# Expert weights asked for in another order, a residual written from ScalarE, and two steps of VectorE exchanged

## The reference

```python
scores = softmax(xf @ gate_w.T)                  # 32 experts
top_w, top_i = lax.top_k(scores, 6)              # 6 experts for each token
h  = silu(xb @ w1[e]) * (xb @ w3[e])             # up: 512 -> 352, twice
ob = h @ w2[e]                                   # down: 352 -> 512
y  = zeros.at[token].add(ob * weight)            # back to the tokens
out = x + y + (silu(xf @ sw1) * (xf @ sw3)) @ sw2   # and a shared expert
```

## Time and profile before

| | us |
|---|---|
| median of 3 runs | 1013.27 |
| lowest and highest | 1009.97, 1017.4 |
| the profiled execution's own time | 1011.21 |
| its span, first to last instruction | 1009.2 |

### The profile page before, as it was taken

How to read it: one execution, slowest core, us unless ns; L and a number is a source line. 1 busy time by engine, 2 the same in 40 slices (tenths; PEclk the granted TensorE clock), 3 DMA queues, 4 the chain that set the end, 5 groups by cost and what they waited for, 6 DMA issues and landing times.

```text
span 1009.2 us, 18358 instructions
## 1 busy us (share of the span) xinstructions
PE 977.7 (97%) x5540; PEld 843.5 (84%) x5541; DVE 694.6 (69%) x1053; ACT 592.6 (59%) x966; POOL 270.8 (27%) x170
## 2 busy tenths in 40 slices
PE   8899899999999999999999999989998999999997
PEld 7788698899888987888888888777877898888885
DVE  5655555675567575778766676656667888778876
ACT  6444576666665665455555552542267788778873
POOL 2200221322132141333333220010015455444441
PEclk9899999999999999899999999999999999999999
DMA  9100263312331413222121103510558999998995
GB/s 317 48 0 1 68 219 106 89 52 67 104 95 59 88 43 115 84 84 83 62 83 62 63 21 134 164 43 1 214 198 261 280 307 331 357 345 283 302 346 173
DMA packets 76143, 145.07 MB, mean 144 GB/s; under 512 B 13540, under 2 KB 41060, under 8 KB 75856
## 3 DMA queue, kind: packets, MB, share of 16 engines
q1 hardware_dynamic: 68256, 132.53, 39.2%
q0 software_dynamic: 7856, 12.16, 5.4%
HBM read 146.86 MB, written 15.07 MB: 160 GB/s over the span
## 4 chain that ended last, share of the span: by engine, by line
PE 75%; DMA 8%; SPq 6%; issue 4%; DVE 4%; ACT 3%; DVEq 0%; ACTq 0%; POOLq 0%
PE ps L327 19%; PE ps L328 19%; PE ps L329 19%; PE ps L719 6%; DMA w_raw<-in_w 3%; SPq L954 2%; PE ps L987 2%; PE ps L786 1%; PE ps L796 1%; DMA w_and_lists<-in_w 1%; PE ps L776 1%; PE ps L999 1%; SPq L1193 1%; DMA y_scratch<-x 1%; DMA wo_raw<-in_owT 1%
## 5 line engine op out<-in xcount | busy, mean ns | idle before, releaser
L1012 DVE TENSOR_TENSOR w_l<-w_raw,w_h 128x1408 fp32r<-128x1408 f32 x76 | 121.7, 1624 | 30.0 <-ACT w_h L1008 21.4
L1008 ACT ACTIVATE w_h<-w_raw 128x1408 fp32r (+1 forms) x76 | 102.7, 1377 | 33.1 <-DMA w_raw<-in_w 30.7
L748 POOL TENSOR_TENSOR lw_l<-lw_raw,lw_h 128x1024 fp32r<-128x1024 f32 x32 | 77.0, 2411 | 145.8 <-ACT lw_h L744 140.6
L327 PE MATMUL ps<-w_h,xeT_h 128*128 128x352 f32 x288 | 97.3, 338 | 3.6 <-DVE w_l L1012 3.1
L328 PE MATMUL ps<-w_l,xeT_h 128*128 128x352 f32 x288 | 93.0, 323 | 0.0
L329 PE MATMUL ps<-w_h,xeT_l 128*128 128x352 f32 x288 | 92.9, 323 | 0.0
L1168 POOL DMA_INDIRECT xe<-xn_scratch,take x37 | 40.7, 1100 | 188.4 <-DVE give L1116 100.9
L1172 POOL DMA_INDIRECT y_scratch<-ob,give x34 | 78.6, 2311 | 18.2 <-issue 9.4
L327 PE MATMUL ps<-xT_hi,lw_h 128*128 128x512 f32 x192 | 78.4, 409 | 0.0
L328 PE MATMUL ps<-xT_lo,lw_h 128*128 128x512 f32 x192 | 77.3, 403 | 0.0
L329 PE MATMUL ps<-xT_hi,lw_l 128*128 128x512 f32 x192 | 76.4, 398 | 0.0
(11 more groups left out here) (328 smaller groups left out, 2739.9 us busy)
## 6 DMA issues: line engine op xcount, KB each, us to landing
w_raw<-in_w SPq DMA_DIRECT2D x78, 704.0 KB
w_and_lists<-in_w SPq DMA_DIRECT2D x39, 512.0 KB
w_and_lists<-in_w SPq DMA_DIRECT2D x39, 192.0 KB
rkB<-rk_scratch SPq DMA_DIRECT2D x56, 128.0 KB, 3.2
wq_raw<-in_Wq SPq DMA_DIRECT2D x8, 512.0 KB, 4.9
wo_raw<-in_Wo SPq DMA_DIRECT2D x16, 256.0 KB, 2.9
lw_raw<-in_kwT SPq DMA_DIRECT2D x8, 512.0 KB, 3.4
lw_raw<-in_qwT SPq DMA_DIRECT2D x8, 512.0 KB, 3.4
```

The costliest lines, as they stand in the source:

```text
L327: nc.tensor.matmul(out_ap, lh, rh, start=first, stop=False)
L748: e.tensor_tensor(lw_l[n][:, :, :], lw_raw[n][:, :, :], lw_h[n][:, :, :], ALU.subtract).then_inc(lw_ready[n], 1)
L1008: e.activation(w13_h[:, k, n, :, :], w13_raw[:, slot(raw), n, :, :], ACT.Copy).then_inc(w13_hi_s, 1)
L1012: e.tensor_tensor(w13_l[:, k, n, :, :], w13_raw[:, slot(raw), n, :, :], w13_h[:, k, n, :, :], ALU.subtract).then_inc(w13_ready, 1)
```

## The change

Three edits, all in the routed stage.

1. **Weights.** SyncE asks for the down weights one item later in its list: up weights of item m+5, then down weights of item m+4. In the loop the four values of the item whose down weights come first in a turn (`kept`) are read again from the table, since they can't be carried over from the turn before.
2. **Residual.** The write of `x` is issued by ScalarE, in its pass 2, behind the same wait for `d_read`.
3. **End.** VectorE makes the low half of the last item's result (`ex_dve_ob_low(e, last_i, 1)`) ahead of all four additions of what was read back, not between the second and the third.

```diff
@@ ex_act
             if isinstance(m, int) and m == 2:
                 e.wait_ge(d_read, NSH)
+                e.dma_start(y_dram[0].ap()[0:T, :].rearrange("(t p) d -> p t d", p=P), x[:, :, :]).then_inc(scratch_io, 16)
@@ block.sync
             ex_load_w13(e, 4, 0, 3, values[4])
-            e.wait_ge(d_read, NSH)
-            e.dma_start(y_dram[0].ap()[0:T, :].rearrange("(t p) d -> p t d", p=P), x[:, :, :]).then_inc(scratch_io, 16)
             values += [ex_values(e, m) for m in range(5, 7)]
             for m in (5, 6):
                 ex_load_w13(e, m, m % 2, m // 2 + 1, values[m])
                 ex_load_w2(e, m - 1, (m - 1) % 2, (m - 1) // 2 + 1, values[m - 1])
-            ex_load_w2(e, 6, 0, 4, values[6])
             with e.Fori(1, last_i - 1) as i:
+                kept = ex_values(e, i * 2 + 4)
                 for k in range(2):
                     values = ex_values(e, i * 2 + (k + 5))
                     ex_load_w13(e, i * 2 + (k + 5), 1 - k, i + (k + 3), values)
-                    ex_load_w2(e, i * 2 + (k + 5), 1 - k, i + (k + 3), values)
+                    ex_load_w2(e, i * 2 + (k + 4), k, i + 3, kept)
+                    kept = values
@@ block.vector
-            for t in range(TT):
-                if t == 2:
-                    ex_dve_ob_low(e, last_i, 1)
+            ex_dve_ob_low(e, last_i, 1)
+            for t in range(TT):
                 e.wait_ge(part_arrived[t], 32)
                 e.tensor_tensor(x[:, t, :], y_back[0][:, t, :], y_back[1][:, t, :], ALU.add).then_inc(y_sum, 1)
```

More of the change, by code:

```diff
@@ L1386, in _ @@
                     ex_load_w13(e, i * 2 + (k + 5), 1 - k, i + (k + 3), values)
-                    ex_load_w2(e, i * 2 + (k + 5), 1 - k, i + (k + 3), values)
+                    ex_load_w2(e, i * 2 + (k + 4), k, i + 3, kept)
+                    kept = values
             for k in range(2):
-                for s, n, uses in ((w13_in[k][0], 16, 3 - k), (w13_in[k][1], 16, 3 - k), (w2_in[k], 32, 3 - k)):
+                for s, n, uses in ((w13_in[k][0], 16, 3 - k), (w13_in[k][1], 16, 3 - k), (w2_in[k], 32, 2)):
                     e.wait_ge(s, last_i * n + uses * n)
```

## The result

| | before | after |
|---|---|---|
| median | 1012.79 us (6 runs) | 1027.69 us (6 runs) |
| lowest and highest | 1009.97, 1017.4 | 1024.78, 1029.85 |
| ratio, 95% interval | | 1.0152 (1.0125 to 1.0179) |
| the profiled execution, its span | 1011.21, 1009.2 | 1028.52, 1026.8 |

The change makes the kernel 1.5% slower, some 15 us; 1015 was forecast, with 1022 as the upper end. Lines behind the first edit have moved by one (954 stays, 1193 is now 1194, 1168 is 1169).

A forecast was written before the change was run, and what follows sets the result against it. TensorE's work was taken to bound the first half, with 6.7 us lost to late up weights in the second. Terms 0 + 2.5 - 0.5 = +2.0 us took the profiled execution from 1011.21 to 1013.2; median forecast 1015, range 1007 to 1022.

The forecast's parts named there:

- a turn of its loop that waits for nothing takes 12.42 us: SyncE's loop: two items take 12.42 us; four added reads, 2.62 us, make it 15.04.
- SyncE becomes the bound: Rival, SyncE's loop: turns of 15.5 us, slower than the DMA, give 1021, with the write's worst case 1024; chance 0.20.
- Term 0 for the weights: Weights edit: one item of lead is given and the added reads eat it, net 0 us.
- bounds of -3 to +6: Weights edit: half the 6.7 us won if reads cost less, 6.0 us more if each read costs 0.77.
- A queue that needs 7.6 us an item can't feed passes of 6.91 whatever the order: Weights' DMA queue against TensorE's passes: argument against the order paying in full.
- from about item 21 on: Weights edit, SyncE's loop: from there each turn's first up weights are just in time.
- the first rival: Order pays in full: reads hidden, 6.7 us of second half and 3.2 of pass 4 gone, 1002.9; chance 0.07.
- The order makes ScalarE late: Down weights land behind the next up weights; ScalarE waits about 1.1 us, put at 0, up to 0.7 a turn.
- Residual, +2.5: Residual's write from ScalarE's queue ahead of pass 4: landing at 763, gathered tokens at 769.1, +2.5 us.
- the estimate of 5.2: Gather of tokens ahead of pass 4: takes 5.2 us in a draining queue.
- the worst case: Residual's write sharing engines with up weights: 11 us on top of 5.0, landing capped at 765, +3.3 to +6.0.
- End, -0.5: VectorE's end: the last low half fits ahead of the additions while VectorE is idle, -0.5 us.

The follow-up runs named there:

- e13: The changed kernel, unaltered, run again on another chip: 1016.11 us, ratio 1.0050 to the kernel before.
- e16: The kernel before with four unused table reads added to each turn of SyncE's loop, run again on another chip: 1016.74 us, ratio 1.0077.
- e5_after_slot0: The changed kernel with SyncE's loop loaded at the first slot of an instruction block: 1022.26 us, ratio 1.0096 to the kernel before.
- e17: The changed kernel, unaltered, run a third time: 1017.01 us, ratio 1.0067 to the kernel before.
- e14_two_loads: The changed kernel, all three edits, with 6 table loads a turn in place of 12, one filling three registers: 1002.43 us, ratio 0.9904 to before.
- e4: The kernel before with the new weight order, its four values carried in registers instead of extra reads: 1008.52 us, ratio 0.9957.
- e7: New weight order on the kernel before, values carried in registers, SyncE's loop loaded at a block's first slot: 1007.37 us, ratio 0.9951.
- e12: The changed kernel with GpSimd's indexed, adding scatter replaced by a plain write: 1017.11 us (one run).
- e9: The kernel before with two unused table reads added at the head of each turn: 1013.24 us, ratio 1.0029.
- e1_order: The kernel before with only the weights edit, new order and its four extra reads a turn: 1029.8 us, ratio 1.0162.
- e3_reads: The kernel before with four unused table reads at the head of each turn, old order: 1031.37 us, ratio 1.0181.
- e2_resid: The kernel before with only the residual's write issued by ScalarE: 1011.91 us, ratio 0.9997.
- e8_end: The kernel before with only the end edit, the last low half ahead of the additions: 1011.0 us, ratio 0.9968.
- e18: The changed kernel with a plain write in place of GpSimd's scatter, run again: 1013.91 us, ratio 1.0029 to the kernel before.
- e11_regs_end_resid: All three edits, the weights' values carried in registers instead of four extra reads: 1007.5 us, ratio 0.9969 to the kernel before.

## Why the prediction was wrong

**The turn of SyncE.** The step that failed is "a turn of its loop that waits for nothing takes 12.42 us" plus four reads, 15.04. The reads were right (15.1 in e13 and e16). The 12.42 was a number of one execution: where SyncE is held the same code takes 13.4, and the changed loop 15.9 to 16.6. I had one trace and took its clean turn for a constant; my own rival "SyncE becomes the bound" put the extra into dearer reads and stopped at a turn of 15.5. By the ratios the hold makes some 9 to 11 of the 15 us: 1.0162 and 1.0152 with it, 1.0050 and 1.0067 without, and for the reads alone 1.0181 against 1.0077. e5_after_slot0, held too, has only 1.0096; if its slot did nothing, the hold's part on that chip is 3 to 5 us. Without the hold the changed kernel would have come to some 1018 to 1020 (an estimate, 1012.8 by those ratios), inside the range and above the 1015; whether a run meets the hold was not mine to foresee from one trace.

**Term 0 for the weights.** Without the hold it is +4.8 us from pass 5 to pass 34 (211.9 against 207.1; e17 has 211.3), inside the bounds of -3 to +6. Item 35 was asked for at 984.11, 3.8 later than worked out.

**"A queue that needs 7.6 us an item can't feed passes of 6.91 whatever the order"** has the pace right and the conclusion wrong. The same 50 us of before and of e14_two_loads, TensorE's busy time first, DMA share and GB/s last:

```profile
930.00:980.00 50.00, 49.15 (x274) 43.17 (x273) 40.44 (x57) 37.18 (x54) 24.20 (x14) 1.00 0.99 328
```

```profile
930.00:980.00 50.00, 49.81 (x280) 44.07 (x278) 40.71 (x56) 38.60 (x55) 24.13 (x14) 1.00 0.98 329
```

The DMA engines are as full in one as in the other. Taken from the updates of their semaphore, the up weights of items 10 to 34, 22 of them new, land every 7.9 us before and every 8.1 us in e14. Yet e14's 29 passes take 201.2 us. What differs is the lead. Item 10's up weights no longer stand behind the wait for the down weights of item 9: they are asked for at 787.26 in e14, at 799.28 before.

```profile
787.26 1.08 SPq L1194 DMA_DIRECT2D w_raw<-in_w  x2
```

Their first half lands 14.9 us ahead of pass 10 in e14 (793.6, the pass starts at 808.5), 3.8 us ahead before (804.3 and 808.1). At item 34 e14 has 3.6 us of lead left (971.6 and 975.2). So the queue does fall behind, and the lead lasts to the end. e13_after_again starts with a lead of 13.9 us too; its turns of 15.1 us leave 4.0 of it at item 20, as the prediction had it ("from about item 21 on"). With that the first rival, the order paying in full (1002.9), was a real possibility for the weights; what closed it were the reads that came with the order.

**The order makes ScalarE late.** The waits for down weights came (22.7 us in 20 waits; some 1.1 each was forecast) and, as put, cost little of themselves: with the values in registers the order gains 4.4 and 5.0 us (e4 and e7).

**The clock** was not in the sum. In 12 of the 19 later traces pass 4 took 8.45 to 9.6 us and not 7.0, a loss of 1.4 to 2.6 us. It is in every kernel of the new order but e7 and e12, and in one of the old order, e9. Why the new order brings it is open: the stall ahead is about as long as before, 3.46 against 3.21 us. Behind pass 5 the clock falls again where SyncE's lateness stalls TensorE: 3.4 us at half clock in after, 6.8 in e1_order and 6.9 in e3_reads, none in e13, e16 and e17. So of the 11.5 us between e3 and e16 in the table up to 3.4 are the clock and not SyncE itself.

**Residual, +2.5.** Measured -0.3 us (0.9997, 0.9975 to 1.0018). The chain of e2_resid, to be held beside the earlier trace rows:

```profile
747.85 10.18 DMA y_scratch<-x
...
758.90 5.06 DMA xe<-xn_scratch,take
```

Against the start of pass 3 (756.26 before, 753.97 here) the write is issued 3.3 us later and lands 2.6 later, not 5.3: it takes 10.2 us as before (10.9), not 12.3. The gather takes 5.1 us and not 7.9, which gives the 2.6 back; here the estimate of 5.2 held. Pass 4 comes 10.04 us behind pass 3, before 10.28. A megabyte alone takes 5.0 us, so the write does share the engines with the weights. That agrees with the Trainium skill ("DMA: Bandwidth & Descriptors", "Queues, rings and completion order"), by which an engine alternates between the queues that have work. What was too dear is my price for it, up to 14.3 us in the worst case.

**End, -0.5.** Measured 0.9968 (0.9940 to 0.9996), but the rows show no gain. VectorE in e8_end:

```profile
993.14 0.75 DVE L1136 SCALAR_TENSOR_TENSOR ob_l<-ps,wl,ob_h 128x512 fp32r<-128x512 f32 x1 [2.68 <-ACT ob_h L1057]
993.99 1.30 DVE L1972 TENSOR_TENSOR x<-xn_c,w_and_lists 128x512 f32<-128x512 f32 x2
996.21 1.33 DVE L1972 TENSOR_TENSOR x<-xn_c,w_and_lists 128x512 f32<-128x512 f32 x2 [0.92 <-DMA w_and_lists<-y_scratch]
```

The low half is out of the way, and then VectorE waits 0.92 us for the third tile read back, which the low half had covered before. From pass 34's start to the first output it is 24.2 us, before 24.1. The 3 us of the ratio are not explained by this; the interval's end lies at 0.4 us. The low half itself takes 0.75 us, where the prediction had 0.49.

## What to carry to other kernels

A sequencer that issues all DMAs is an engine with a busy time: before adding a register load to its loop, hold its clean turn beside what one turn has to feed, and leave a margin, since the same turn was 8% longer in other executions. Try an order apart from what it costs to carry out: here the order alone was worth 0.4% and its four table loads a turn cost 0.8 to 1.8%, until the values came in registers or three in one load. And a queue slower than the passes that it feeds needn't cost anything as long as the lead lasts: count the lead at the start and what each pass takes off it, beside the pace.

## What was not expected of the hardware

- In after and on the two chips of e1 to e8 SyncE stands still in nearly every pass, in pieces of 0.3 to 0.7 us between 0.9 and 2.7 us behind GpSimd's start of an indirect gather; in before and on the three chips of e9 to e18 it doesn't. It adds about 1 us to a turn of 12.4 or of 15.1 us (two passes). Where SyncE has slack nothing comes of it: from pass 5 to 34 the kernel before takes 207.1 us without the hold, e8_end 207.2 with it.
- A table load into one register takes 0.27 us and, with what follows it, 0.65 until the next. Six loads fewer a turn, with three of the six left going into three registers each, took the clean turn from 15.1 to 11.8 us (e13 and e14). The Trainium skill ("Runtime: NRT & Kernel Launch", section on instruction fetch mechanics) gives about 200 ns a register even in bulk. The load into three registers took 0.72 us in the median of e14's trace, 0.24 a register, so the load itself roughly agrees, and most of the saving is in the steps around it.
- At pass 4 TensorE came out of stalls of 0.6 to 3.2 us at full clock in some executions (e7_regs_slot0 to before) and at half clock behind stalls of 1.8 to 3.9 us in others (e18_plain_again to e11_regs_end_resid); a stall's length alone doesn't decide it.
